# Two stores of a layer-0 recurrence step issued at another place of ScalarE's order

## The reference

```python
q = _causal_dwconv_silu(x @ Wq.T, qcw, qcb)          # likewise k (scaled) and v
a = sigmoid(x @ Wa.T + ba)                           # the gates, one per value channel
beta = sigmoid(x @ Wb.T + bb)                        # one per head
def step(S, inp):
    err = einsum('bhij,bhj->bhi', S, kt) - vt
    S = at[..., None] * S - bt[..., None, None] * (err[..., None] * kt[:, :, None, :])
    o = einsum('bhij,bhj->bhi', S, qt)
```

## Time and profile before

| | us |
|---|---|
| runs | 6992.06, 6990.51, 6972.95 (median 6990.51) |
| profiled execution, its own time | 6996.25 |
| its span | 6994.4 |
| DVE busy in the span | 5329.3 (76%) |
| PE busy | 5171.4 (74%) |
| POOL busy | 3451.6 (49%) |
| ACT busy | 3332.5 (48%) |

### The profile page before, as it was taken

One profiled execution on the slowest core, in us unless ns is written; L12 is line 12 of the kernel. 1 busy time (PEld: TensorE's weight loads), 2 busy tenths in 40 slices (PEclk: granted clock), 3 DMA queues, 4 the chain that ended last, 5 costly groups with the idle time before them and its releaser, 6 DMA issues. The chain is left out here.

```text
span 6994.4 us, 177868 instructions
## 1 busy us (share of the span) xinstructions
PE 5171.4 (74%) x59191; PEld 3349.9 (48%) x59191; DVE 5329.3 (76%) x15729; ACT 3332.5 (48%) x7298; POOL 3451.6 (49%) x4488
## 2 busy tenths in 40 slices
PE   3677767777777777777777727888888888888888
PEld 2455555555555555555555513444444444344343
DVE  4888988888888888888888856666666666666665
ACT  4445555455554455555455513444444444444444
POOL 1777877777777777777777751111111111111110
PEclk9777777777777777777777758888888888888888
DMA  4555555555555555555555531111111111111111
GB/s 163 136 131 136 139 141 144 133 134 134 139 142 138 131 134 139 141 139 138 125 141 141 140 82 46 46 45 45 45 46 46 46 47 45 45 45 45 45 46 34
DMA packets 1195973, 695.80 MB, mean 99 GB/s; under 512 B 1054936, under 2 KB 1106808, under 8 KB 1193593
## 3 DMA queue, kind: packets, MB, share of 16 engines
q1 hardware_dynamic: 888044, 500.99, 27.2%
q10 hardware_dynamic: 307200, 185.09, 11.0%
HBM read 371.99 MB, written 313.95 MB: 98 GB/s over the span
## 5 line engine op out<-in xcount | busy, mean ns | idle before, releaser
L1855 DVE TENSOR_REDUCE nmax<-w_bank 128x1 f32<-128x512 f32 x1024 | 642.8, 684 | 406.2 <-PE w_bank L1437 401.5
L941 DVE SCALAR_TENSOR_TENSOR p_bank<-y,conv_w,p_bank 128x128 f32<-128x128 f32 x3072 | 819.7, 350 | 117.1 <-ACT p_bank L753 82.3
L535 POOL TENSOR_TENSOR qp<-qp,ab 128x512 f32<-128x512 f32 (+7 forms) x1024 | 871.7, 851 | 75.2
L540 POOL TENSOR_TENSOR qp<-qp,pt 128x512 f32<-128x512 f32 (+7 forms) x1024 | 839.4, 820 | 80.3
L677 PE MATMUL p_bank<-xnT,wqkv 128*128 128x128 f32 x4096 | 699.3, 341 | 67.0 <-ACT xnT L838 56.3
L677 PEld LDWEIGHTS p_bank<-xnT,wqkv 128*128 128x128 f32 x4096 | 652.5, 250 | 144.7 <-issue 144.7
L1392 POOL TENSOR_TENSOR ot<-ot,ln_w 128x1024 f32<-128x1024 f32 x64 | 151.0, 2359 | 1136.0 <-ACT ot L1694 1136.0
L537 POOL TENSOR_TENSOR pt<-qp,vb 128x512 f32<-128x512 f32 (+7 forms) x1024 | 696.1, 680 | 10.9 <-DVE vb L998 10.9
L1397 POOL TENSOR_TENSOR x1b<-x,bias 128x256 f32<-128x256 f32 x64 | 46.4, 726 | 1172.4 <-DVE bst L1951 1172.4
L1668 ACT ACTIVATE pt<-e_bank 128x1024 f32<-128x1024 f32 x512 | 514.0, 1021 | 181.1 <-PE e_bank L1467 179.7
L612 PE MATMUL d_bank<-st 64*32 64x80 f32 x16384 | 442.0, 267 | 109.8 <-issue 70.3
(11 more groups left out here) (234 smaller groups left out, 11326.5 us busy)
## 6 DMA issues: line engine op xcount, KB each, us to landing
prod_dram<-prod ACTq DMA_DIRECT2D x64, 1280.0 KB, 9.0
kp<-prod_dram SPq DMA_DIRECT2D x64, 640.0 KB, 5.6
qp<-prod_dram SPq DMA_DIRECT2D x64, 640.0 KB, 7.2
a_dram<-at ACTq DMA_DIRECT2D x64, 512.0 KB
ab<-a_dram SPq DMA_DIRECT2D x64, 512.0 KB, 5.9
v_dram<-vt ACTq DMA_DIRECT2D x64, 512.0 KB
vb<-v_dram SPq DMA_DIRECT2D x64, 512.0 KB, 4.6
vt<-e_dram SPq DMA_DIRECT2D x64, 512.0 KB
```

The source lines that it names most:

```text
L535: link(nc.gpsimd.tensor_tensor(q, q, ab[:, g, r:r + 1, :].to_broadcast([128, w, DV]), ALU.mult), 1)
L540: link(nc.gpsimd.tensor_tensor(q, q, pt2[:, 0:w], ALU.add))
L941: nc.vector.scalar_tensor_tensor(out=zz, in0=y[:, j % Y_BANKS, i, :, tap:tap + C], scalar=conv_w[:, m, tap:tap + 1], in1=zz, op0=ALU.mult, ...
L1855: nc.vector.tensor_reduce(nmax[:, n:n + 1], bank[:], AX.X, ALU.max, negate=True).then_inc(freed, 1)
```

## The change

The stores of the gates and of the betas of step s + 2 are issued by ScalarE directly behind `crossed(s)`, ahead of SiLU of banks 4 and 5, in place of behind the eviction of bank 0. Nothing else moves; the functions called are the same.

```diff
                 if valid(lo, hi):
                     crossed(s, n, g)
+                if ahead:
+                    store_gates(s + 2, n + 1, g)
+                    store_betas(s + 2, n + 1, g)
                 if front:
                     silu(s + 1, 1 - g, 4)
                     silu(s + 1, 1 - g, 5)
...
                     products(s + 1, n + g, 1 - g)
                 if ahead:
                     evict(s + 2, g, 0)
-                    store_gates(s + 2, n + 1, g)
-                    store_betas(s + 2, n + 1, g)
                 if front:
                     key_rows(s + 1, 1 - g)
```

## The result

The change makes the kernel slower: 7094.97 us median (7092.08 to 7108.09) against 6991.28 before (6972.95 to 7001.33), ratio 1.0155 with a 95% interval of 1.013 to 1.018. That is 104 us more. The times given are medians of all executions; one execution of experiment 8 took 10115 us, and it counts in the median given there but not in the ratio. The profiled execution of the changed kernel has a span of 7106.2 us against 6994.4. Lines on VectorE are one number higher in it than before (L941 is L942, L964 is L965, L981 is L982).

A forecast was written before the change was run, and what follows sets the result against it. DVE was taken as nearly the bound, beside a second chain through x stores and `xk`. Terms -20 (stall), 0 (issues) and +19 (collision) summed to -1 us: 6990 us against the median, range 6955 to 7034.

The forecast's parts named there:

- the collision rival: At the `xk` load from `x_dram`: the collision costs 1 us a step or more, giving 7024 us; chance 0.25.
- What bounds: Recurrence: DVE nearly the bound, 89% busy, beside a second chain between the halves through x stores and `xk`.
- The stall removed: ScalarE's issue stall before `kt`: removing it shortens DVE's tap group 3 wait by 0.38 us a step; -20 us taken.
- The limit by `kp`: Load of `kp`, next late: takes 3.1 of the 18.1 us gain, unless it lands up to 1.2 us sooner.
- the wait of L941 on ACT: DVE's wait for convolution banks: a sign of being right if below 3 us in total in 3000.
- The extra gain that a rival hoped for: PE earlier with the decays DVE waits for: another 12 us, in the mostly-gain case of 6955 us; chance 0.27.
- The issues on ScalarE: Two issues between second x store and SiLU of bank 4: 0.93 us together, covered by waiting for DVE; cost 0.
- The collision: Gates' store overlapping the `xk` load on the DMA queues: 0.4 us delay, 0.75 of it counting; +19 us.
- The far bound: Upper limit of the `xk` load's delay by the gates' store: 2.6 us, from the `vb` load's 6.8 us landing.
- The rule on turn-taking: DMA engines serve queues packet by packet in turn; gates' packets would alternate with `xk` packets, fitting the 0.44 share.
- The clock: PE idles longer, so cross products run at the lower clock: 13 us lost, 7003 us; chance 0.06.
- the stall that moves: Gates' store issue takes 4 us at the new place too, delaying SiLU of bank 4: 7050 us; chance 0.04.

The follow-up runs named there:

- experiment 8: Half the gates' store and the betas' store behind the cross results, the other half behind the v store; 6981.93 us against 6981.98 for the kernel before.
- the two versions without collision or a new stall: Against the kernel before: gates' store issued by SyncE at its slot's end, ratio 0.9946; both stores directly behind the betas, ahead of the cross results, 0.9959.
- experiment 5: The changed kernel with the gates' 128 rows stored in plain order, so gates are permuted; 7020.72 us against 6981.3 for the kernel before.
- experiment 6: The changed kernel with SyncE loading `xk` only once the gates' store has landed too; 7175.66 us against 6972.92 for the kernel before.
- experiments 1 and 7: Against the kernel before: only the gates' store moved to the change's place, ratio 1.0138; both stores moved behind the v store, ratio 1.0021.

## Why the prediction was wrong

The forecast was no change, with -20 us and +19 us; the measured time, 7095, is above the range (6955 to 7034). The side was that of the collision rival, which had 0.25 and a price that was also too small (7024).

- *What bounds.* Right: DVE with a second chain through the x stores and `xk`. Of a 2.5 us longer median landing the gap between the halves took 2.16, a part of 0.86, where I used 0.75 in the forecast and 0.85 in the rival.
- *The stall removed.* Right in mechanism and size. The issue takes 0.587 us, tap groups 0 to 8 are 0.44 us a step shorter (forecast 0.31 to 0.38; the 19.2 us that went are 0.40), and the two versions without collision or a new stall gain 0.41% and 0.54%, 23 and 27 us of medians, against the 20 forecast. The limit by `kp` did not show: its landing fell to 4.8 us, as the text had allowed. Two signs were not quite as I put them: the wait of L941 on ACT reads 7.5 us and not below 3, all of it the loop's turn, and PE's new wait in front of its projections is for ScalarE's `xnT` and not for DVE's taps. The extra gain that a rival hoped for did not come either: DVE's wait for the decays is 51.1 us in place of 36.2.
- *The issues on ScalarE.* Right: 0.59 and 0.35 us, covered by DVE's taps.
- *The collision.* This term failed. "Overlaps the first 1.1 us or so of the `xk` data", "takes 0.44 of the DMA engines", "hence a delay of about 1.1 x 0.44 = 0.5 us": measured 2.5 us (4.2 to 6.7), which with 0.86 and 62 steps makes 133 us in place of 19; less the 27 us of the 0.44, that is close to the 104 measured. The factor was wrong: the share of 0.44 is not all engines half busy but, as experiment 5 and the stretches at 0.47 to 0.49 suggest, half of the engines at work all the time. The load is complete when the slower half is, so what counts is the store's whole rest on those engines and not its share of all. The overlap was probably too short as well. The store lands 3.3 us after the x stores (experiment 6), and in the slot of the earlier trace rows the data of `xk` starts about 1.1 us after its issue (share 0.11 in 2056.0 to 2056.5, 0.86 in the next half microsecond); by these two the rest is at most 2.2 us, and less by the unknown time between last data and landing, where I had 1.1. An estimate with the whole rest fits: 2.2 us for 512 KB, 1.1 for 384 and none for 256 (1.1 us for each 128 KB), against 2.07, 0.79 and -0.08 us measured as growth of the mean from the issue of `xk` to half 1.
- *The bounds.* The far bound, 2.6 us from the `vb` landing of 6.8, was nearly the truth. I took a value near the other end since the overlap looked short. The range should have held this bound: 2.6 x 0.85 x 62 - 20 = 117 us, 7107. The inner range of the forecast has a slip: terms of 15 and 35 us give 7010 and not 7008, which changes nothing.
- *The rule on turn-taking.* I weighed the turn-taking of packets but took it to agree with the share of 0.44. No run here shows whether packets take turns. The rule that experiment 5 cites from the Trainium skill (DMA: Bandwidth & Descriptors, section "Why a DMA increments its semaphore by 16 and not by 1"), on how many engines a DMA runs on, would have said that this share has to be read as 8 engines of 16.
- *The clock and the stall that moves.* The mean granted clock over 500 to 3500 is 0.76 before and after, and the cross products to `xk` stayed (9.42 and 9.52): neither happened in the change. A stall on ScalarE did show at another store in experiments 1 and 7, and in the change SyncE got one (decay stores).

Not settled: what the betas' store adds behind the gates (6.3 and 6.7 us of landing); and the half of the engines itself. The dose and the waiting load show that the store in flight makes `xk` late, but no run puts the same slow store on engines that `xk` does not use. Nor is the DMA share a strict one: in stretches of half a microsecond it reaches 1.29 in the `xk` load before the change (2058.0 to 2058.5), so a share near 0.5 is a hint that wants a second sign, as experiment 5 gives.

## What to carry to other kernels

Before moving a store, look at what is loaded right behind its new place and ask if that load is waited for; a store nobody waits for can cost more than the engine stall it removes. Read a DMA share near 0.5 as possibly half of the engines at full load: a load over all engines is done when the shared half is. A gap in the DMA share on the timeline (here between the errors' load and the first x store) is the place for such a store, and a kernel's own order of independent issues is the cheapest thing to try there.

## What the runs showed of the hardware

- The price of a store in flight is free room and then a slope: 256 KB in front of `xk` cost nothing in the mean time from its issue to half 1, 384 KB 0.87 us, 512 KB 2.15 (each with the betas' 8 KB; against 4.67 us with the betas alone). The median landing alone (4.2, 4.3, 4.9, 6.7 us) makes the slope look like a step.
- An issue of 8 KB took 4.42 us behind a 1280 KB store of 320-byte pieces, and 2.47 us behind two stores of 512 KB in rows, in place of 0.34. SyncE's 16 KB issues took 1.80 us behind the slow `xk` load, in place of 0.60. What holds the engine is what is ahead in its queue, not the size of what is issued.
- The same 512 KB in the same 4 KB rows moved at a DMA share up to 0.93 (262 GB/s, with the x stores' end in it) in place of 0.49 (129 GB/s), by the order of dimensions alone. The faster store is not free: with it the x stores beside it landed 1.1 us later than in the change (10.66 and 9.52 us from the cross products to `xk`).
